# Weighted expert rows added by the scatter straight into the output, with six groups of output rows stored before the experts

## The reference, cut to what matters

```python
h = tok(x)                                    # 16 x 65 x 128 from image patches, plus class token
h = concatenate([h, txt], axis=1)             # 16 x 193 x 128: 3088 tokens of 128 features
h = h + attn(layernorm(h))                    # linear attention and a 3-tap convolution
xt = layernorm(h)                             # from here on: the expert layer
shared = silu(xt @ sw1) * (xt @ sw3) @ sw2    # for every token
scores = xt @ gate_w.T                        # 8 experts
idx = top_k(scores + biases, 2)               # the two experts of a token
p = sigmoid(top_k(scores, 2)); p = p / sum(p) # their two weights
y_e = silu(xt @ w1[e]) * (xt @ w3[e]) @ w2[e] # needed for chosen experts alone
out = h + shared + p[0] * y_idx0 + p[1] * y_idx1
```

## Time and profile before

| | |
|---|---|
| three runs | 261.74, 262.54, 262.74 us, median 262.54 us |
| profiled execution | 263.96 us, of which the span of the record is 262.1 us |
| busy share of the span | PE 89%, DVE 72%, ACT 59%, POOL 43% |
| chain that ended last | PE 77%, DVE 12%, ACT 5%, ACT's queue 2%, issue 2% |
| HBM | 22.80 MB read, 9.03 MB written |

### The profile page before, as it was taken

How to read it: one execution, slowest core, us unless ns; L and a number is a source line. 1 busy time by engine, 2 the same in 40 slices (tenths; PEclk the granted TensorE clock), 3 DMA queues, 4 the chain that set the end, 5 groups by cost and what they waited for, 6 DMA issues and landing times.

```text
span 262.1 us, 5589 instructions
## 1 busy us (share of the span) xinstructions
PE 232.5 (89%) x1491; PEld 191.2 (73%) x1491; DVE 189.7 (72%) x737; ACT 155.3 (59%) x436; POOL 113.3 (43%) x121
## 2 busy tenths in 40 slices
PE   0499599999999999998898997999999999999930
PEld 0477578787878787876666665888888888888720
DVE  1543957888888888898997877766666666665892
ACT  0335436676767676776984326666666666666390
POOL 1300000027373737270457640566666666767500
PEclk9999759999999999999999999999999999999995
DMA  7999941416161601010011413323333333339657
GB/s 217 318 320 356 323 168 17 171 17 217 37 211 30 227 21 43 21 40 10 24 42 50 128 37 74 82 72 103 84 86 86 94 83 87 87 82 281 160 136 191
DMA packets 31422, 31.68 MB, mean 121 GB/s; under 512 B 4323, under 2 KB 27404, under 8 KB 30497
## 3 DMA queue, kind: packets, MB, share of 16 engines
q1 hardware_dynamic: 25960, 23.95, 30.9%
q0 software_dynamic: 3392, 6.36, 7.4%
q10 hardware_dynamic: 2040, 1.04, 1.4%
HBM read 22.80 MB, written 9.03 MB: 121 GB/s over the span
## 4 chain that ended last, share of the span: by engine, by line
PE 77%; DVE 12%; ACT 5%; ACTq 2%; issue 2%; DVEq 0%
PE bank L1574 15%; PE bank L1286 12%; PE bank L1594 10%; PE bank L1301 6%; PE bank L1583 5%; PE bank L1493 3%; PE bank L1374 3%; PE bank L1563 2%; PE bank L1478 2%; PE bank L1378 2%; PE bank L1481 2%; PE bank L1300 2%; PE bank L1334 2%; DVE sh_h L1059 2%; PE bank L1332 2%
## 5 line engine op out<-in xcount | busy, mean ns | idle before, releaser
L782 POOL DMA_INDIRECT xs_dram<-xd,pos_i x50 | 55.0, 1100 | 85.1 <-DVE pos_i L971 72.3
L793 POOL DMA_INDIRECT y_dram<-att,goal x56 | 55.1, 983 | 36.9 <-ACT att L719 36.6
L1286 PE MATMUL bank<-wt,xp_both 128*128 128x128 f32 x288 | 38.8, 289 | 0.0
L1286 PEld LDWEIGHTS bank<-wt,xp_both 128*128 128x128 f32 x288 | 37.3, 203 | 1.3 <-issue 0.4
L705 ACT ACTIVATE att<-bank 128x256 f32<-128x256 f32 x56 | 21.4, 383 | 24.4 <-PE bank L1574 23.6
L1594 PE MATMUL bank<-w_sb,att 128*128 x224 | 34.5, 277 | 0.0
L1196 DVE CAST xsT_h<-bank 128x128 fp32r<-128x128 f32 x56 | 16.3, 291 | 24.2 <-PE bank L1563 24.2
L1594 PEld LDWEIGHTS bank<-w_sb,att 128*128 128x128 f32 x224 | 29.4, 191 | 0.3 <-issue 0.2
L1574 PE MATMUL bank<-xp_both,xsT_h 128*128 x56 | 26.8, 478 | 0.7 <-DVE xsT_l L1198 0.7
L1209 DVE TENSOR_TENSOR att<-att,bank 128x256 f32<-128x256 f32 x56 | 23.0, 410 | 1.7 <-ACT att L705 1.7
L1574 PE MATMUL bank<-xp_both,xsT_l 128*128 x56 | 22.2, 396 | 0.0
(11 more groups left out here) (204 smaller groups left out, 496.6 us busy)
## 6 DMA issues: line engine op xcount, KB each, us to landing
xp_both<-in_patches SPq DMA_DIRECT2D x7, 1152.0 KB
xs_all<-xs_dram SPq DMA_DIRECT2D x56, 64.5 KB, 1.9
xd<-y_dram SPq DMA_DIRECT2D x8, 384.0 KB, 4.7
w<-in_w SPq DMA_DIRECT2D x2, 1024.0 KB, 9.5
y_dram<-att,goal POOLq DMA_INDIRECT x56, 2.3
xs_dram<-xd,pos_i POOLq DMA_INDIRECT x50
hrow<-in_txt SPq DMA_DIRECT2D x2, 384.0 KB, 10.2
out_tokens<-hrow SPq DMA_DIRECT2D x6, 128.0 KB, 2.0
```

What stands on the lines that cost most here:

```text
L782: nc.gpsimd.indirect_dma_start(out=xs_dram[:, :], out_offset=bass.IndirectOffsetOnAxis(ap=pos_i[0:rows, j, k:k + 1], axis=0), in_=xd[0:row ...
L793: nc.gpsimd.indirect_dma_start(out=y_dram[:, :], out_offset=bass.IndirectOffsetOnAxis(ap=goal[u][:, 0:1].bitcast(I32), axis=0), in_=ys[u][ ...
L1286: M(ps[:, 0:D], xp[p][:, k, :], wt[:, k, :], start=(k == 0), stop=False)
```

## The change

**Weights.** Each group's sigmoids are taken on ACT (`sigmoids(g, step)`: exp(-s), ln(1 + ..), exp(-..), three instructions), in the main loop, and DVE's new `weights(g)` writes the two normalised weights beside the token rows (column D + 1 of `xd`, so a row has 130 numbers). `positions(g)` loses the two reductions that put the smaller position first. The weight travels through `xs_dram`, and ACT multiplies by it in the copy that it made of each result anyway.

**Scatter out.** POOL's indirect DMA of a result adds (`compute_op=ALU.add`) into output rows instead of writing into `y_dram`. For groups 0 to 5 these are the true output rows; so `hrow` with its shared part must lie there before, and `store_whole` stores chunks 0, 1 and 2 (two groups each) ahead of the experts. POOL waits for these stores before its first result. For groups 6, 7 and CLS the sums go to rows behind the output, which POOL fills with zeros early. Since an add reads and writes, two of them must not meet on one row: POOL waits before tile t until the DMA of tile t - 3 has landed, and, if a flag is set, until that of tile t - 1 has. The flag is computed from the counts: it is set unless each expert's rows are spread so that two tiles in a row, or two apart, can't hold the same token.

**Tail.** After all 56 DMAs SP loads the sums of groups 6 and 7 (two DMAs of 128x3x128) and CLS; DVE adds them with three instructions; five stores follow.

```diff
-ROW = D + 1
-BIG = 1 << 20
+ROW = D + 2
+LATE = 18
+PADS = 4
+UNUSED = TILES - -(-2 * NTOK // P)
+ACC = NTOK + PADS * P
+NROWS = ACC + (CLS - LATE) * P + B
 U = 8
...
-    xs_dram = nc.dram_tensor("xs_dram", [E * CAP + P, ROW], F32).ap()
-    y_dram = nc.dram_tensor("y_dram", [2 * NID, D], F32).ap()
+    xs_dram = nc.dram_tensor("xs_dram", [E * CAP + UNUSED * P, ROW], F32).ap()
+    out_rows, out = out, out[0:NTOK, :]
...
+            def store_whole(c, first, step):
+                sp.wait_ge(sh_add, 2 * c + 2)
+                for dst, src in out_views(c)[first::step]:
+                    sp.dma_start(dst, src).then_inc(out_sent, 16)
+
...
             sp.wait_ge(pad_set, 2)
-            sp.dma_start(xs_dram[E * CAP:, :], pad).then_inc(padded, 16)
+            for i in range(UNUSED):
+                sp.dma_start(xs_dram[E * CAP + P * i:E * CAP + P * i + P, :], xs[1 + i % (PADS - 1)]).then_inc(padded, 16)
+            store_whole(0, 0, 1)
...
+            store_whole(1, 0, 1)
...
+            store_whole(2, 0, 2)
...
-            for k in range(2):
-                for u in range(U):
-                    sp.wait_ge(y_sent[u], needed[k][u])
-                for c, (a, b) in enumerate(CHUNKS):
-                    rows = rows_of(a)
-                    sp.dma_start(y_rows[0:rows, k, a:b, :],
-                                 y_dram[k * NID + a * P:k * NID + a * P + rows * (b - a), :].rearrange(
-                                     "(j q) d -> q j d", q=rows)).then_inc(y_loaded[k][c], 16)
-
-            for turn, c in enumerate(FINISHED):
-                sp.wait_ge(fin_done, turn + 1)
-                for dst, src in out_views(c)[0::(1 if c < 2 else 2)]:
-                    sp.dma_start(dst, src).then_inc(out_sent, 16)
             for u in range(U):
-                sp.wait_ge(y_sent[u], 16 * (TILES // U))
-            sp.wait_ge(out_sent, 16 * sum(len(out_views(c)) for c in range(len(CHUNKS))))
+                sp.wait_ge(y_sent[u], 16 * (1 + TILES // U))
+            for i in range(2):
+                sp.dma_start(acc[:, 3 * i:3 * i + 3, :], out_rows[ACC + 3 * P * i:ACC + 3 * P * i + 3 * P, :].rearrange(
+                    "(j q) d -> q j d", q=P)).then_inc(acc_loaded[i], 16)
+            sp.dma_start(acc[0:B, CLS - LATE, :], out_rows[NROWS - B:NROWS, :]).then_inc(acc_loaded[2], 16)
+            sp.wait_ge(fin_done, 2)
+            for dst, src in out_views(3)[0::2]:
+                sp.dma_start(dst, src).then_inc(end_sent, 16)
+            sp.wait_ge(out_sent, 16 * sum(len(out_views(c)) for c in range(3)))
+            sp.wait_ge(end_sent, 16 * sum(len(out_views(c)) for c in range(3, len(CHUNKS))))
...
+            def sigmoids(g, step):
+
+                a, b = 3 * g, (J if g == G - 1 else 3 * g + 3)
+                act.wait_ge((sc_done, ea_done, la_done)[step], g + 1)
+                if step == 0:
+                    A(sg[0][:, a:b, :], sc[:, a:b, :], ACT.Exp, scale=-1.0).then_inc(ea_done, 1)
+                if step == 1:
+                    A(sg[1][:, a:b, :], sg[0][:, a:b, :], ACT.Ln, bias=1.0).then_inc(la_done, 1)
+                if step == 2:
+                    A(sg[2][:, a:b, :], sg[1][:, a:b, :], ACT.Exp, scale=-1.0).then_inc(sg_done, 1)
+
...
             shared_silu(2, 1)
-            act.wait_ge(x2_turned, G)
-            nc.scalar.copy(x2T[:, 3 * P * (G - 1):3 * P * (G - 1) + 3 * P + B], bank[6][:, 0:3 * P + B]).then_inc(x2T_done, 1)
-            round_w13(5)
-            act.wait_ge(gate_done, G)
-            nc.scalar.copy(sc[:, 3 * (G - 1):CLS, :], bank[6][:, GATE_AT:GATE_AT + 3 * E].rearrange("p (j e) -> p j e", e=E))
-            nc.scalar.copy(sc[0:B, CLS, :], bank[6][0:B, GATE_AT + 3 * E:GATE_AT + 4 * E]).then_inc(sc_done, 1)
             act.wait_ge(x2_done, G + 1)
             for j in tiles_of(G - 1):
                 rows = rows_of(j)
                 nc.scalar.copy(xd[0:rows, j, 1, 0:D], xd[0:rows, j, 0, 0:D]).then_inc(twice_done, 1)
+            act.wait_ge(x2_turned, G)
+            nc.scalar.copy(x2T[:, 3 * P * (G - 1):3 * P * (G - 1) + 3 * P + B], bank[6][:, 0:3 * P + B]).then_inc(x2T_done, 1)
+            act.preload_act_table_set("natural_log_exp_and_others")
+            act.wait_ge(gate_done, G)
+            nc.scalar.copy(sc[:, 3 * (G - 1):CLS, :], bank[6][:, GATE_AT:GATE_AT + 3 * E].rearrange("p (j e) -> p j e", e=E))
+            nc.scalar.copy(sc[0:B, CLS, :], bank[6][0:B, GATE_AT + 3 * E:GATE_AT + 4 * E]).then_inc(sc_done, 1)
+            for step in range(3):
+                sigmoids(G - 1, step)
+            act.preload_act_table(ACT.Silu)
+            round_w13(5)
...
-            act.wait_ge(top_done, 1)
-            A(sg[:], by_slot[:], ACT.Exp, scale=-1.0).then_inc(sg_done, 1)
-            act.preload_act_table(ACT.Silu)
+            act.wait_ge(sh_add, EARLY)
+            for dst, src in out_views(2)[1::2]:
+                act.dma_start(dst, src).then_inc(out_sent, 16)
...
-                after(act, y_sent[buf], 16 * (n - 1 if u < 2 else n))
-                nc.scalar.copy(ys[buf][:], bank[6 + q][:, 0:D]).then_inc(ys_done[at], 1)
+                use = n - 1 if u < 2 else n
+                if use > 0:
+                    act.wait_ge(y_sent[buf], 16 * (1 + use))
+                A(ys[buf][:], bank[6 + q][:, 0:D], ACT.Copy, scale=goal[buf][:, 1:2]).then_inc(ys_done[at], 1)
...
+            for u in range(U):
+                a, b = (NROWS - NTOK) // P * u // (U - 1), (NROWS - NTOK) // P * (u + 1) // (U - 1)
+                if u < U - 1:
+                    rows = out_rows[NTOK + P * a:NTOK + P * b, :].rearrange("(j q) d -> q j d", q=P)
+                    blank = pad[:, 0:D].rearrange("p (j d) -> p j d", j=1).broadcast_to([P, b - a, D])
+                else:
+                    rows, blank = out_rows[NROWS - B:NROWS, :], pad[0:B, 0:D]
+                pool.dma_start(rows, blank).then_inc(y_sent[u], 16)
+            pool.wait_ge(ids_ready, 2)
...
+            flag_reg, turn_reg, lag = (pool.alloc_register(n) for n in ("flag", "turn", "lag"))
+            pool.wait_ge(flag_done, 1)
+            pool.reg_load(flag_reg, flag[0:1, 0:1])
+            pool.wait_ge(out_sent, 16 * sum(len(out_views(c)) for c in range(3)))
+            for u in range(U):
+                pool.wait_ge(y_sent[u], 16)
             for t in range(TILES):
                 u = t % U
+                if t > 0:
+                    if t % U == 1:
+                        pool.reg_alu(turn_reg, flag_reg, 16 * (1 + t // U), ALU.add)
+                        pool.reg_alu(lag, turn_reg, 16, ALU.max)
+                    pool.wait_ge(y_sent[(t - 1) % U], lag)
+                    pool.sem_inc(paced, 1)
+                if t >= 3:
+                    pool.wait_ge(y_sent[(t - 3) % U], 16 * (2 + (t - 3) // U))
 
                 pool.wait_ge(ys_done[t % SLOTS], t // SLOTS + 1)
                 nc.gpsimd.indirect_dma_start(
...
-                    out=y_dram[:, :],
+                    out=out_rows[:, :],
                     out_offset=bass.IndirectOffsetOnAxis(ap=goal[u][:, 0:1].bitcast(I32), axis=0),
-                    in_=ys[u][:], in_offset=None, bounds_check=bound, oob_is_err=False).then_inc(y_sent[u], 16)
+                    in_=ys[u][:], in_offset=None, compute_op=ALU.add).then_inc(y_sent[u], 16)
 
...
-                V.tensor_reduce(pos_2[:, a:b, :], prod[:, a:b], AX.X, ALU.add).then_inc(slots_done, 1)
-                dve.wait_ge(slots_done, g + 1)
                 with nc.allow_low_precision(reason="whole numbers below 2 ** 24"):
-                    V.tensor_reduce(pos_i[:, a:b, 0], pos_2[:, a:b, :], AX.X, ALU.min)
-                    V.tensor_reduce(pos_i[:, a:b, 1], pos_2[:, a:b, :], AX.X, ALU.max).then_inc(pos_done, 1)
+                    V.tensor_reduce(pos_i[:, a:b, :], prod[:, a:b], AX.X, ALU.add).then_inc(pos_done, 1)
+
+            def weights(g):
+
+                a, b = 3 * g, (J if g == G - 1 else 3 * g + 3)
+                dve.wait_ge(sg_done, g + 1)
+                for j in tiles_of(g):
+                    last = V.max(raw8[:, j, :], sg[2][:, j, :])
+                then(last)
+                then(V.tensor_tensor(mx[:, a:b], raw8[:, a:b, 0], raw8[:, a:b, 1], ALU.add))
+                then(V.reciprocal(mx[:, a:b], mx[:, a:b]))
+                V.tensor_tensor(xd[:, a:b, :, D + 1], raw8[:, a:b, 0:2],
+                                mx[:, a:b].rearrange("p (j k) -> p j k", k=1).broadcast_to([P, b - a, 2]), ALU.mult)
 
...
+                    weights(i - 2)
                     positions(i - 2)
...
-            raw_best(G - 1)
-            then(V.tensor_tensor(swap[:], ix8[:, :, 0], ix8[:, :, 1], ALU.is_gt))
-            dve.wait_ge(raw_done, J)
...
+            V.tensor_scalar(full[:], tf[:], float(P), None, ALU.mult)
+            cut = bank[6][:, CUT_AT:CUT_AT + 2 * E].rearrange("p (k e) -> p k e", k=2)
+            for k in range(2):
+                last = V.tensor_scalar(cuts[:, 2 + k, :], cut[:, k, :], float(P * (k - 2)), None, ALU.add)
```

(101 more changed lines are left out.)

134 lines of the change are left out of this document (52 added, 82 removed).

## The result

The changed kernel takes 281.59 us (median of 4, 280.71 to 284.25), the kernel before, timed beside it, 262.40 (261.74 to 262.74): ratio 1.074, 95% interval 1.069 to 1.078. It is slower by 19.2 us where 3.6 less were predicted. The profiled execution took 280.71, its span is 278.9.

What follows compares the result with a forecast made beforehand. PE was taken to bound loop and experts, with DVE, ACT and DMAs setting the tail's end. Loop +1.0, routing +0.2, experts 0 and tail -4.8 gave -3.6, so 258.9 us; 8 in 10 range 257.2 to 262.0.

Steps and rivals of the forecast that it cites:

- the paragraph *Experts: Expert tiles: POOL's adding DMAs issue in 0.98 to 1.1 us, hidden under PE's 1.47 a tile; cost 0.
- the issue could do the same, from 1.17 us an instruction on: Rival in the experts: POOL's issue of adding DMAs sets the pace; chance 0.16 together with the slow landing.
- the slow landing: Rival in the experts: landing three tiles back sets the pace, gain gone at 4.6 us; 0.16 together with slow issue.
- The landing: Experts: an adding DMA lands in 3.2 us, between 2.3 and 4.2, which stays under PE's 1.47 a tile.
- The flag: Experts: expected clear; rival that it is set, each DMA waiting for the one before, +95 us, chance 0.01.
- The loop: Main loop: new DVE work makes PE 0.2 us late in each of five turns, +1.0; bounds nothing and +2.5.
- Between loop and experts: Stretch from loop to first expert: DVE delays and ACT's table load, less savings, +0.2 us; bounds -0.3 and +0.9.
- The tail: After the experts: DVE's multiply-adds go, fewer stores, DVE waits for `shared_down`; -4.8 us, bounds -5.2 and -3.5.
- a sign of being wrong: Tail: prediction wrong if DVE waits there for the loads of the sums rather than for `shared_down`; no size given.
- The sum: Whole kernel: +1.0 + 0.2 - 4.8 = -3.6 us, from a median of 262.54 to 258.9.

Runs made afterwards that it cites:

- experiment 1: The changed kernel with its 56 result DMAs writing instead of adding, all else kept: 259.08 us, ratio 0.988 to the kernel before.
- Experiment 5: The changed kernel with plain-writing result DMAs and without the weights' work on ACT and DVE (weight column set to 1): 258.09 us, ratio 0.988 to the kernel before.
- experiment 2: The kernel before with its result DMAs adding into a y_dram filled with zeros early, no waits for earlier tiles: 282.64 us, ratio 1.076 to the kernel before.

## Why the prediction was wrong, step by step

**The step that failed** is the issue in the paragraph *Experts*: "should an added row need half as much work again or twice as much, 0.98 becomes 1.1. Bounds: 0.98, and 1.1; the fixed part is taken as equal." Shown in its place: 1.56 us, of which the fixed part grew by 0.4 and a row costs 2.3 to 2.7 ns instead of 1.0. Even twice the price per row would have stayed below the 1.17 at which POOL becomes the bound; the fixed part took it over. The two rows I had (128 and 16 rows of a plain scatter) give a price per row of the plain form and can say nothing of the fixed part of another form; a bound drawn from them was no bound. The rival "the issue could do the same, from 1.17 us an instruction on" was the case, held at 0.16 together with the slow landing, because its price came from the same two rows.

**The landing** was right: 3.3 us where 3.2 was taken, and it sets no pace. The Trainium skill, "DMA: Bandwidth & Descriptors", section "Rules for kernel authors", has an accumulating DMA read its destination and write it later; landings of 2.2 without the add (experiment 1) and 3.3 with it agree. That rule had drawn my attention to the landing, when the cost was in the issue.

**The flag** was clear: POOL never waited for the DMA one tile back, its gap stayed 0.30.

**The loop**: +0.2 a turn predicted, +0.20 measured (13.36 against 13.16), over the five turns from `sums(1)` (43.59 and 45.98) to `sums(6)` (110.59 and 111.81) 67.00 against 65.83: +1.17. Experiment 5 shows the cause, the wait of `sums` for DVE.

**Between loop and experts**: +0.2 predicted. From `sums(7)` (121.71 and 123.01) to the first result (165.11 and 165.05) it took 43.40 instead of 42.04: 1.36 longer, above my upper bound of 0.9. PE's granted clock fell to half for some 3 us there (128 to 132) in the changed kernel and not in the kernel before. Such a fall happens without the change too, and costs about 1.7 us there: experiment 2, which has the old routing, had such a fall and took 44.27 (granted clock 0.96), while its forms with 64 rows and with half rows, which are the same up to this point (but for one more DMA of zeros in the second), had none and took 42.58 each (1.00). Experiment 1 had one too (44.45, clock 0.96); experiment 5, without the weights' work, had none (42.23). What the edits themselves cost here, with the clock at 1.00, no run shows. SP's loads started at 156.13 and 156.04, so after `sums(7)` they came 1.39 later: the whole loss lies ahead of them.

**The tail**: -4.8 predicted, -5.1 measured, though not by the way I had worked out; that the numbers are close is luck. I had DVE wait for `shared_down`; in the changed kernel that was over before the last result was issued, and DVE waited 7.5 us for the landing and the loads of the sums. I had named this as a sign of being wrong; it costs nothing, since POOL's lateness moved the shared layer under the experts. In experiment 1, where POOL isn't late, the tail goes as I had worked it out. DVE waits for `shared_down` of the class tokens, and its three adds follow without a wait for the sums:

```profile
256.46 0.28 DVE L1106 TENSOR_TENSOR hrow<-bank,hrow 16x128 f32<-16x128 f32 x1 [0.78 <-PE bank L1482]
256.78 0.28 DVE L1251 TENSOR_TENSOR hrow<-hrow,xd 16x128 f32<-16x128 f32 x1
256.99 1.01 DVE L1255 TENSOR_TENSOR hrow<-hrow,xd 128x384 f32<-128x384 f32 x2
```

From the first result (169.07) to the end (261.3) it took 92.2 us, the kernel before 97.1 (165.05 to 262.1): -4.8 for experts and tail together, as predicted.

**The sum** without the failed step stands: 258.9 predicted, 259.08 measured in experiment 1. Against the kernel before beside it that is 2.9 less, where 3.6 were predicted.

## What to carry to other kernels

An instruction of another kind needs a measured price of its own: a slope from its sibling bounds what grows with size, and nothing else. Before trading engine work for one DMA feature, add up how often the issuing engine would pay: here 0.6 us, 56 times, on an engine that had 0.17 us a tile to spare, against 5 us saved once. Experiment 2 shows the cheap way to such a price: the old kernel with the new kind of instruction alone, which one profile settles.

## What the runs showed of the hardware, unexpected

- POOL's issue of an adding DMA: indirect 1.55 us for 128 rows, 1.40 for 64, 1.27 for 16; plain 0.96; direct 0.86 with and 0.54 without the add; the bytes of a row don't matter.
- The program did not end until 9.1 to 9.3 us after POOL's last DMA issue in the two kernels that stored from POOL late, though their data had landed 3.4 and 5.0 us before the end. What runs in that time no record shows. If the distance is the same in other kernels, which only these two show, the kernel before would need some 256.0 for it, and it binds nothing; the changed one, whose last issue ended at 269.1, would need some 278.3 of its 278.9, so its tail could hardly have become shorter. No kernel here ended sooner after POOL: experiment 1 has 9.5 us.
- At the start, PE's granted clock fell to half after PE had waited 1.38 us for DVE ahead of `sums(0)` (and, in the kernel before, 1.35 for ACT behind it), for a time that differs between executions of either kernel. Windows of PE from 30 to 40 us, the kernel before, then the changed one (the column behind POOL is the clock):

```profile
30.00:40.00 10.00, 8.98 (x30) 7.04 (x30) 6.07 (x27) 4.11 (x10) 0.00 (x0) 0.51 0.57 193
```

```profile
30.00:40.00 10.00, 9.89 (x54) 8.02 (x54) 9.29 (x42) 5.52 (x16) 0.00 (x0) 0.85 0.89 293
```

It put `sums(1)` 2.4 us earlier in the changed kernel's profile, and so hid what loop and routing cost. Experiment 1's profile has the long form (0.53) and starts that stage at 46.4: the luck isn't the change's. Two single profiles should be compared stage by stage with the clock beside them, never by their spans alone.
